# A gated cross-attention block on one core: maxima moved between units, the row turned one unit earlier, an inverse on another engine, two banks signalled apart

## The reference, cut to what matters

```python
x = x + tanh(g_xattn) * xattn(layernorm(x), ctx)   # 16 sequences of 100 rows, ctx 16 x 1444 x 96
x = x + tanh(g_ffn) * ffn(layernorm(x))            # self-attention and a router with 8 experts and a shared one
# xattn, per sequence b, 16 heads of 64:
q, k, v = x @ w_q, ctx @ w_k, ctx @ w_v
attn = softmax(q @ k.T / 8)        # 100 x 1444 for each head
out = (attn @ v) @ w_o + b_o
```

## Time and profile before

| | |
|---|---|
| runs, median | 1360.14 us |
| profiled execution | 1361.45 us |
| its span (first to last instruction) | 1359.7 us |
| TensorE busy | 1254.0 us, 92% |
| VectorE busy | 978.6 us, 72%, 1762 instructions |
| ScalarE busy | 825.2 us, 61% |
| GpSimd busy | 680.0 us, 50%, 555 instructions |
| the power on GpSimd (L594), x31 | 52.0 us, mean 1678 ns |
| mean granted TensorE clock | 0.98 of full speed |

### The profile page before, as it was taken

The page is one execution under the profiler, slowest core; times in us unless marked ns, Lnnn a source line. Parts: engine busy times, 40 slices in busy tenths (PEclk is TensorE's granted clock), DMA queues, the critical chain, the costliest instruction groups (busy, mean ns, idle before and its releaser), DMA issues.

```text
span 1359.7 us, 34631 instructions
## 1 busy us (share of the span) xinstructions
PE 1254.0 (92%) x14472; PEld 910.3 (67%) x14472; DVE 978.6 (72%) x1762; ACT 825.2 (61%) x1476; POOL 680.0 (50%) x555
## 2 busy tenths in 40 slices
PE   6689799999899999999999999998999999889998
PEld 4356576767677676767676767676767676667776
DVE  5778486868686868676777767676868686966766
ACT  1336465766666666666666666675666666655664
POOL 3125455455555545455555555555455554634554
PEclk9779799999999999999999999999999999999999
DMA  6201603030303020211103130303030200010000
GB/s 167 63 1 20 175 13 78 13 78 13 76 13 74 12 72 15 52 40 38 52 15 76 14 78 13 78 13 78 13 78 13 62 13 15 7 21 1 8 8 13
DMA packets 122277, 57.27 MB, mean 42 GB/s; under 512 B 108262, under 2 KB 117706, under 8 KB 122122
## 3 DMA queue, kind: packets, MB, share of 16 engines
q1 hardware_dynamic: 122122, 55.07, 17.7%
HBM read 15.38 MB, written 0.82 MB: 12 GB/s over the span
## 4 chain that ended last, share of the span: by engine, by line
PE 68%; DVE 13%; ACT 12%; issue 4%; DMA 2%; SPq 1%; POOL 0%; DVEq 0%; POOLq 0%; ACTq 0%
PE psum L756 16%; PE psum L737 8%; PE psum L837 8%; PE psum L738 7%; PE psum L739 7%; PE psum L772 5%; DVE p_lo L430 4%; DVE mx L1285 3%; PE psum L869 3%; ACT p_hi L966 3%; PE psum L784 3%; ACT p L965 3%; PE psum L882 3%; PE psum L891 2%; ACT p L960 2%
## 5 line engine op out<-in xcount | busy, mean ns | idle before, releaser
L430 POOL TENSOR_TENSOR p_lo<-p,p_hi 128x768 f16<-128x768 f32 (+1 forms) x144 | 261.3, 1815 | 331.5 <-ACT p_hi L961 212.6
L1285 DVE TENSOR_REDUCE mx<-psum 128x1 f32<-128x512 f32 (+1 forms) x585 | 358.3, 650 | 50.0 <-PE psum L837 43.5
L960 ACT ACTIVATE p<-psum 128x768 f32<-128x768 f32 (+1 forms) x256 | 214.9, 839 | 260.9 <-PE psum L739 260.8
L756 PEld LDWEIGHTS psum<-c_both,p_hi 128*128 128x128 f16 x4992 | 281.9, 99 | 87.0 <-issue 36.4
L756 PE MATMUL psum<-c_both,p_hi 128*128 128x97 f16 (+1 forms) x4992 | 324.0, 207 | 7.5 <-ACT acc_sb L976 7.4
L737 PE MATMUL psum<-qk_hi,cT_both 97*128 97x384 f16 (+1 forms) x768 | 259.1, 337 | 22.7 <-DMA qk_hi<-mrow 8.8
L430 DVE TENSOR_TENSOR p_lo<-p,p_hi 128x768 f16<-128x768 f32 (+1 forms) x240 | 267.5, 1114 | 12.5 <-ACT p_hi L961 10.7
L738 PE MATMUL psum<-qk_lo,cT_both 96*128 96x384 f16 (+1 forms) x768 | 258.1, 336 | 0.0
L739 PE MATMUL psum<-qk_hi,cT_both 96*128 96x384 f16 (+1 forms) x768 | 255.8, 333 | 0.0
L837 PE MATMUL psum<-cT_both,qk_hi 96*128 96x512 f16 (+1 forms) x585 | 208.3, 374 | 40.0 <-DVE mx L1285 29.5
L965 ACT ACTIVATE p<-psum 128x384 f32<-128x384 f32 (+1 forms) x256 | 130.0, 508 | 149.8 <-PE psum L739 148.4
(11 more groups left out here) (201 smaller groups left out, 2108.8 us busy)
## 6 DMA issues: line engine op xcount, KB each, us to landing
c_both<-c_new SPq DMA_DIRECT2D x16, 768.0 KB, 3.9
ctx_nat<-in_ctx_dram SPq DMA_DIRECT2D x16, 528.0 KB
aT<-a_new SPq DMA_TRANSPOSE x64, 2.9
wg<-in_L_ffn_e_gate_dram SPq DMA_DIRECT2D x1, 1024.0 KB, 5.5
wu<-in_L_ffn_e_up_dram SPq DMA_DIRECT2D x1, 1024.0 KB, 7.8
wd<-in_L_ffn_e_down_dram SPq DMA_DIRECT2D x8, 128.0 KB, 5.6
out_dram<-x SPq DMA_DIRECT2D x4, 200.0 KB
x<-in_x_dram SPq DMA_DIRECT2D x1, 600.0 KB
```

The costliest lines, as they stand in the source:

```text
L430: engine.tensor_tensor(p_lo[0:m, i % 3, 0:w], p32[0:m, i % 3, 0:w], p_hi[0:m, i % 3, 0:w], ALU.subtract).then_inc(lo_made(b, i)[0], 1)
L756: t = mm(psum[:, ACCB + bank, k * (C + 1):k * (C + 1) + wide], p[0:m, i % 3, n * P:(n + 1) * P], c[parity][0:m, j, 0:wide], start=(j == 0 ...
L960: a(to32, src, ACT.Exp, scale=DH ** -0.5)
L1285: v.tensor_reduce(mx[:, rt, part:part + 1], bank[:, 0:w], AX.X, ALU.max)\
```

## The change

The greedy hand-out of maxima sees 0.7 more load in units 4 and 5, and unit 21 gets none any more; the counts in units 3 to 21 become 2 2 3 2 3 2 1 3 2 1 2 1 2 2 3 2 4 2 0. "m" goes from unit 22 to unit 21. With a maximum in unit 9, "f1" (q, k and v of the self-attention) is cut into that unit's middle third. The inverse of the sums leaves GpSimd's `normalise` and becomes `sums_inverse` on VectorE, in unit 2 for half 1 of the batch before and in unit 14 for half 0, each ahead of that unit's `probs_rest`; it waits there for both copies of the sums. `acc_evac` signals after each of its two instructions, and `pv_unit` waits for each bank where it first writes it. The constant -1 is gone.

```diff
+    for i in (4, 5):
+        load[i] += .7
+    share = {i: 0 for i in range(3, 21)}
-    share = {i: 0 for i in range(3, 22)}
...
-    plan[22].append(("m", 0))
+    plan[21].append(("m", 0))
...
-                pool.wait_ge(acc_out, at + 1)
-                g.tensor_tensor(acc_rc[:, 0:n], acc_sb[:, 0:n, C], minus_one[:, 0:n], ALU.pow).then_inc(acc_rcp, 1)
...
-                if j == 0 and not (isinstance(b, int) and b == 0 and i == 0):
-                    pe.wait_ge(acc_out, b * 2 + i // CH)
...
                         bank, k = divmod(n, PER_BANK[half])
+                        if j == 0 and k == 0 and p is p_hi and c is c_hi and (b or half):
+                            pe.wait_ge(acc_out, (b * 2 + half - 1) * 2 + bank + 1)
...
-                    ins = a(acc_sb[:, t0:t1, :], psum[:, ACCB + bank, 0:(t1 - t0) * (C + 1)].rearrange(
-                        "p (k c) -> p k c", c=C + 1), ACT.Copy)
-                ins.then_inc(acc_out, 1)
+                    a(acc_sb[:, t0:t1, :], psum[:, ACCB + bank, 0:(t1 - t0) * (C + 1)].rearrange(
+                        "p (k c) -> p k c", c=C + 1), ACT.Copy).then_inc(acc_out, 1)
...
+            def sums_inverse(at):
+                n = TILES[at % 2]
+                dve.wait_ge(acc_out, (at + 1) * 2)
+                v.reciprocal(acc_rc[:, 0:n], acc_sb[:, 0:n, C]).then_inc(acc_rcp, 1)
...
                     run_aux(aux, one, b, kind, parity)
+                    if i == 2 and kind != "first":
+                        sums_inverse(b * 2 - 1)
+                    if i == ACC0_AT:
+                        sums_inverse(b * 2)
                     if i and i - 1 not in LO_POOL:
                         probs_rest(dve, v, b, i - 1)
```

More of the change, by code:

```diff
@@ L187, in flamingo_kernel @@
     SET_POOL = ["-1/2", "zero ident", "ident", "zero ident16", "ident16", "zero c_new", "ones c_new", "ones end",
-                "pad qk_hi0", "pad qk_hi1", "lnr0", "minus one", "pad p_hi", "pad p_lo", "mx", "ones v9", "ones mask",
+                "pad qk_hi0", "pad qk_hi1", "lnr0", "pad p_hi", "pad p_lo", "mx", "ones v9", "ones mask",
                 "mask above", "head_mask", "zero a_new", "n1"] + [f"rank of {e}" for e in range(E)] + \
@@ L235, in flamingo_kernel @@
         acc_rc = sb("acc_rc", [P, TILES[1]])
-        minus_one = sb("minus_one", [P, TILES[1]])
         a_new = sb("a_new", [P, 2, TILES[1], P], F16)
@@ L570, in _ @@
             token_rstd(0)
-            step("minus one", g.memset(minus_one[:, :], -1.0))
             step("pad p_hi", g.memset(p_hi[:, :, PW:], 1.0))
@@ L797, in aux @@
                     if n == 1:
-                        pe.wait_ge(acc_out, B * 2)
+                        pe.wait_ge(acc_out, B * 4)
                     if n == 3 * EU:
@@ L1349, in _ @@
             hi, lo = (a_new[:, k, 0:n, 0:C] for k in range(2))
-            dve.wait_ge(acc_out, at + 1)
-            v.reciprocal(acc_rc[:, 0:n], acc_sb[:, 0:n, C]).then_inc(acc_rcp, 1)
+            sums_inverse(at)
             dve.wait_ge(at_in, at * 32)
```

## The result

The changed kernel takes 1349.2 us as a median of four runs (1348.5 to 1351.2) against 1360.17; the ratio is 0.9917 (95% interval 0.9891 to 0.9943). The profiled execution took 1348.50, its span 1346.8. Faster, as forecast, but by 11 us (0.8%) and not by 26: the time lies near the first rival (1352), and outside the forecast's own range (1328 to 1341).

What follows compares the result with a forecast made beforehand. TensorE, busy 92% of the span, was taken as the bound. Terms -0.18 - 0.13 - 2.11 + 0.57 = -1.85 us for each of 13 batches, 27.1 with the ends, gave 1334 us; own range 1328 to 1341, wider range 1328 to 1355.

Steps and rivals of the forecast that it cites:

- the first rival: GpSimd gets ahead of VectorE in unit 5: units 4 and 5 gain only 0.66 us, 1352 in all; chance 0.20.
- What bounds the kernel: TensorE, busy for 92% of the span; the question is where it stands still in a batch's 71.2 us.
- the four stops: TensorE's stops per batch: unit 0 (0.87 us), unit 2's sums (0.62), maximum 3 in unit 4 (1.02), maximum 6 in unit 5 (1.31).
- Row in unit 21: Turning the row in unit 21 hides its DMAs; units 21 to 0 shrink, units 19 and 20 grow: -0.18 us a batch.
- Banks: Signalling unit 2's two banks of sums one by one moves three matmuls out of the way: -0.13 us a batch.
- Inverse: Inverse of the sums on VectorE, 0.20 us each; GpSimd starts its unit 4 remainder as data come; worth nothing by itself.
- Units 4 and 5: With fewer maxima and VectorE ahead of GpSimd, the two units take 5.33 us instead of 7.44: -2.11 a batch.
- Where the maxima go: Maxima moved to units 7, 9 and 10 and q/k/v to unit 9 cost +0.57 us a batch, between 0 and +1.8.
- The ends: Savings outside batches 2 to 14: batch 1 2.2 us, batch 0 0.5, the last batch 0.3.
- Rivals 2, 3 and 4: VectorE first in some batches (1344, 0.07); unit 6 loses the gain (1358, 0.07); VectorE bounds units 7 to 11 (1374, 0.06).
- rival 3: In unit 6 the product waits for the turned sums' DMA and the gain is lost, about 1358; chance 0.07.

Runs made afterwards that it cites:

- b_banks: Kernel before the change with only the two banks of sums signalled one by one; 1358.19 us, ratio 0.9978.
- a_delay1: Changed kernel with one single-column memset on GpSimd between the arrival of its data and its remainder of unit 4; 1349.77 us, ratio 0.9925.
- a_order: Changed kernel with one wait more: GpSimd takes its remainder of unit 4 only after VectorE's of unit 3; 1331.72 us, ratio 0.9785.
- c_pow22: a_order with two maxima back in unit 21, one fewer in units 4 and 10 each, row turned mid unit 22, inverse as GpSimd power; 1327.92 us.
- a_delay2: Changed kernel with two one-column memsets on GpSimd ahead of its remainder of unit 4; 1351.96 us, ratio 0.9949.
- a_predtt: Changed kernel with one GpSimd memset before its unit 4 remainder and a one-column tensor_tensor on VectorE before its unit 3 remainder; 1351.01 us, ratio 0.9929.

## Why the prediction was wrong, by its own steps

- *What bounds the kernel.* Right: the four stops were the ones that moved, and the period carried most of the time (batches 2 to 14: 926.41 to 917.93 us).
- *Row in unit 21.* Forecast 7.41 us for the three turns of ScalarE, measured 7.35; units 19 and 20 took 0.21 and 0.22 more (forecast 0.44). The row leaves at 487.15, 5.2 us before unit 0's second half, and nothing waits for it.
- *Banks.* Forecast -0.13, measured 2.91 to 2.71 us for unit 2, about -0.2; b_banks alone has the same. The product begins at 498.04 and no longer shows a wait of 0.45.
- *Inverse.* Its direct cost is nothing, 31 reciprocals more of 0.19 us. What it moves was seen rightly, GpSimd's start with its data, and called worth nothing by itself; beside the new shares it was what lost the 18.6 us.
- *Units 4 and 5: the step that failed.* Forecast 5.33 us and -2.11, measured 6.84 and -0.60. The step reads "I take VectorE first". The two starts were foreseen 0.03 us apart and came 0.11 apart, because remainder 2 took 1.02 and not 0.94, held by the tail of GpSimd's third product. But at 0.03 to 0.05 VectorE is held too (a_delay1, all 13 middle batches), so the 0.03 foreseen would most likely have lost as well. I had carried over an order from pairs with another GpSimd instruction; the only pairs of the kernel before in which GpSimd ran its remainder just ahead were those at 0.38 to 0.48, and in all of them VectorE was held. With the order forced (a_order) the same sum holds: units 4 and 5 take 5.44 us where 5.33 was forecast, a period 69.21 where 69.35 was, and the kernel 1331.7 us where 1334 was.
- *The first rival* gave 6.78 us for the two units and 1352 in all; 6.84 and 1349.2 came, so its mechanism is the one that the runs show.
- *The Trainium skill*, page "SBUF — State Buffer", section "Who interferes with whom", has the first to issue keep the port. The runs agree for this pair, if issue is read by the stamps: GpSimd first at 0.04, 0.10 and 0.11 us ahead, VectorE first at 0.12 ahead. For GpSimd's products the stamps give no such order (0.08 went both ways). I set the rule aside for what those pairs showed.
- *Where the maxima go.* Forecast +0.57 in units 7 to 11; from the starts of the second halves +0.53. Unit 8's half-filled wait was free as said.
- *The ends.* Forecast 3.0 us, measured 4.5: prologue 0.96 (51.85 to 50.89; in the other runs it ends between 49.3 and 51.9), batch 0 2.14, batch 1 2.46, less 1.09 in the last batch and the experts. Batch 1's stop shrank by 0.8 (9.12 to 8.32) and not by 2.1; what else was saved there was not taken apart. The last line of the sum mixes two starts: 27.1 us off the median of 1360.14 is 1333, not 1334.
- *Rivals 2, 3 and 4* did not come: VectorE was held in all 13 middle batches, and nothing waited in unit 6 or in units 7 to 11 beyond what was forecast. c_pow22 shows that rival 3's place is real, but with GpSimd's power in the way.

## What to carry to other kernels

When a schedule turns on which of two engines takes a shared port, don't forecast the order from start stamps a tenth of a microsecond apart: price both orders, and give most of the chance to the bad one unless a semaphore fixes it. If one of the two has slack, make it wait; that wait was worth 17 us in the kernel before, more than the whole change (11). Taking work off an engine moves its next instruction earlier, and the first thing to ask is what that one will then collide with.

## What the runs showed of the hardware

A stop of TensorE can cost twice. In a_delay1 each middle batch has the same 1.76 us stop in unit 5, but batches 4, 9 and 14 last 72.33 us and the others 70.5 to 70.8. Windows of batch 4 around the stop (us, busy of each engine with counts, granted TensorE clock, DMA share, GB/s), then of batch 3 at the same place:

```profile
369.00:370.00 1.00, 0.96 (x11) 0.88 (x12) 1.00 (x2) 0.00 (x0) 1.00 (x1) 0.61 0.00 0
370.00:373.00 3.00, 3.00 (x21) 1.74 (x19) 1.37 (x3) 0.20 (x1) 0.24 (x1) 0.56 0.00 0
```

```profile
298.50:302.00 3.50, 3.50 (x53) 2.96 (x52) 2.12 (x5) 1.51 (x2) 1.05 (x1) 1.00 0.00 0
```

After the stop the granted clock is 0.61 and then 0.56, near the lower of its two levels (1.2 of 2.4 GHz): 21 matmuls in 3 us where 53 ran in 3.5, and 1.65 us lost once more. The same came in one middle batch of a_delay2 (batch 6) and of a_predtt (batch 11), right behind the same stop, and in none of the profiled run of the changed kernel, whose stop is 1.68 us. What sets these batches apart was not found. The runs of a_delay1 spread from 1346.2 to 1357.4 us, wider than any other here. The profiled one is the slowest, and its three batches account for 5.0 of the 7.6 us by which it is over the median; for the spread of the others this is not shown.
